# A two-layer attention and FFN kernel on one Trainium2 core: eight unread matmuls at its start, another order of the first head pair, and the fourth query projection of each grouped pair moved behind the first value products

## The reference, cut to what matters

```
x = x + xattn(layernorm(x), ctx)     # 32 heads of 128, RMS norm inside, position bias, mask, softmax; returns hidden + out
x = x + ffn(layernorm(x))            # silu(gate) * up, 1376 wide, down
x = x + grouped(layernorm(x), ctx)   # 32 query heads, 8 key/value heads, rope, 30*tanh(l/30), mask, softmax
x = x + lora(layernorm(x))           # W plus the fold of eight rank-16 pairs, bias
```

## Time and profile before

| | |
|---|---|
| runs | 1738.42, 1744.41, 1743.58 us; median 1743.58 |
| the profiled execution | 1740.23 us, its span 1738.4 us |
| mean granted TensorE clock | 0.987 |
| busy share | PE 96%, PE weight load 83%, DVE 52%, POOL 39%, ACT 37% |
| DMA | 74.99 MB, 43 GB/s over the span |

### The profile page before, as it was taken

The page is one execution under the profiler, slowest core; times in us unless marked ns, Lnnn a source line. Parts: engine busy times, 40 slices in busy tenths (PEclk is TensorE's granted clock), DMA queues, the critical chain, the costliest instruction groups (busy, mean ns, idle before and its releaser), DMA issues. The chain is left out here.

```text
span 1738.4 us, 26186 instructions
## 1 busy us (share of the span) xinstructions
PE 1677.0 (96%) x9412; PEld 1449.2 (83%) x9412; DVE 912.4 (52%) x1462; ACT 642.2 (37%) x1757; POOL 685.3 (39%) x480
## 2 busy tenths in 40 slices
PE   8899999999999999999989998799999999999997
PEld 7788888888888888888868886688888788888875
DVE  5734454443544434443454346556657556665674
ACT  5422233221332223332222222455546545564550
POOL 4532343333433324433253433445435434443524
PEclk9999999999999999999989999899999999999998
DMA  5111100111101111011011110201011110010011
GB/s 177 52 52 51 51 20 32 51 51 51 46 5 51 51 51 51 0 51 57 1 51 50 47 38 25 65 31 37 31 38 43 44 37 31 25 43 25 24 38 49
DMA packets 30898, 74.99 MB, mean 43 GB/s; under 512 B 5776, under 2 KB 10256, under 8 KB 30832
## 3 DMA queue, kind: packets, MB, share of 16 engines
q1 hardware_dynamic: 30832, 74.10, 12.2%
HBM read 71.99 MB, written 2.10 MB: 43 GB/s over the span
## 5 line engine op out<-in xcount | busy, mean ns | idle before, releaser
L1761 POOL TENSOR_TENSOR g_swapped<-g_swapped,rawB 128x512 f32<-128x512 f32 x80 | 103.5, 1295 | 159.3 <-ACT g_swapped L1545 159.3
L631 ACT COPY x_pT<-banks 128x512 f32<-128x512 f32 x64 | 37.5, 586 | 337.6 <-PE banks L485 337.6
L920 POOL TENSOR_TENSOR wtV_lo<-rawV,wtV_hi 128x1024 fp32r<-128x1024 f32 x16 | 38.5, 2406 | 309.6 <-ACT wtV_hi L643 309.6
L55 PE MATMUL banks<-wtV_hi,cT_lo 128*128 128x256 f32 x512 | 145.1, 283 | 0.0
L57 PE MATMUL banks<-wtV_hi,cT_hi 128*128 128x256 f32 x512 | 144.8, 283 | 0.0
L56 PE MATMUL banks<-wtV_lo,cT_hi 128*128 128x256 f32 x512 | 144.7, 283 | 0.0
L934 POOL TENSOR_TENSOR x_probs<-x_probs,x_inv 128x512 f32<-128x512 f32 x64 | 66.8, 1044 | 158.0 <-DVE x_inv L769 155.1
L55 PE MATMUL banks<-wtV_hi,g_att_lo 128*128 128x512 f32 x256 | 106.2, 415 | 8.1 <-DVE g_att_lo L1659 8.1
L777 DVE COPY x_v<-banks 128x512 f32<-128x512 f32 x60 | 41.5, 692 | 127.7 <-PE banks L57 127.7
L623 ACT ACTIVATE x_probs<-x_probs,x_top 128x128 f32<-128x128 f32 x256 | 99.2, 390 | 18.8 <-DVE x_top L760 18.8
L801 DVE TENSOR_TENSOR resid<-banks,resid 128x512 f32<-128x512 f32 x128 | 84.1, 686 | 40.0 <-PE banks L57 40.0
(11 more groups left out here) (226 smaller groups left out, 4953.2 us busy)
## 6 DMA issues: line engine op xcount, KB each, us to landing
rawV<-in_x_wV SPq DMA_DIRECT2D x16, 512.0 KB, 4.3
rawO<-in_x_wO SPq DMA_DIRECT2D x16, 512.0 KB, 6.0
rawO<-in_g_wQ SPq DMA_DIRECT2D x16, 512.0 KB, 3.2
rawV<-in_g_wO SPq DMA_DIRECT2D x16, 512.0 KB, 3.2
rawA<-in_x_wA SPq DMA_DIRECT2D x15, 512.0 KB, 6.3
rawB<-in_x_wB SPq DMA_DIRECT2D x15, 512.0 KB, 5.0
rawA<-in_f_gu SPq DMA_DIRECT2D x5, 512.0 KB, 3.7
rawB<-in_f_gu SPq DMA_DIRECT2D x5, 512.0 KB, 3.1
```

The lines of the kernel that those rows point to most:

```text
L55: pe.matmul(out, w[1], x[0], start=start, stop=False)
L631: nc.scalar.copy(pT[:, j, :], banks[:, TURN_BANK + j, :]).then_inc(pT_ready, 1)
L920: pool.tensor_tensor(wt[kind][1][:, :], raw[kind][:, :], f32(wt[kind][0][:, :]), ALU.subtract)\
L1761: pool.tensor_tensor(part, part, sin[:, :].unsqueeze(1).to_broadcast([P, HB, P]), ALU.mult)\
```

## The change

It has three parts. At the start, TensorE's list gets eight matmuls whose result nobody reads; the two last context chunks are cut ahead of the key weights of head 1, and the value weights ahead of the copies of the first keys; `turn_x` goes ahead of each `values_of`. In the first head pair, SyncE loads V and B ahead of the bias; `add_hidden` goes from VectorE to ScalarE (between the last `keep_values`/`high` and `exps(0, 0)`), GpSimd's `twice_of` goes ahead of the mask and gets one more operation (a sign), `inverse(0, 0)` goes ahead of `logits(0, 1)`, and GpSimd's low parts of V and B go, in every `body`, from its end behind `bias(a, 0)`. In the grouped attention, the fourth query projection goes behind `turn` 3, and the lists of ScalarE and VectorE follow.

```diff
 SyncE, first attention, body:
                     load("A", g)
-                    bias(g)
                     load("V", g)
                     load("B", g)
+                    bias(g)
                     load("O", g)
 TensorE, start:
+                def warm(n):
+                    for _ in range(n):
+                        pe.matmul(banks[:, 4, :], wqk("A", 0, 1, 0), wt["A"][0][:, half_of(1)], start=True, stop=True)
                 def start():
                     pe.wait_ge(key_hi["A"], 1)
+                    warm(WARM)                       # WARM = 8
                     pe.wait_ge(key_lo["A"], 1)
...
                     for n in range(4):
-                        values_of(n, V0 + n)
                         turn_x(2 * n)
                         turn_x(2 * n + 1)
+                        values_of(n, V0 + n)
 ScalarE, start:
                     key_half("A")
-                    context(0)
-                    context(1)
+                    for c in range(DC):
+                        context(c)
                     key_half("B")
-                    context(2)
-                    context(3)
+                    weights("V", 0)
                     for half in range(2):
                         keep(k_[:, 0, half * HALF:(half + 1) * HALF], K_A0 + half)
-                    weights("V", 0)
                     scale_x(0)
                     scale_x(1)
...
                     for n in range(4):
+                        high(2 * n)
+                        high(2 * n + 1)
                         if n < 3:
                             scale_x(2 * n + 2)
                             scale_x(2 * n + 3)
...
                         keep_values(n)
-                        high(2 * n)
-                        high(2 * n + 1)
+                    for b in range(B):
+                        add_hidden(b)                # scalar.activation(.., Identity, bias=mean_scaled, scale=twice)
 VectorE, start:
                     logits(0, 0)
-                    for b in range(2):
-                        add_hidden(b)
+                    inverse(0, 0)
                     logits(0, 1)
                     query(Q_B0, 0, 1)
-                    inverse(0, 0)
-                    for b in range(2, 4):
-                        add_hidden(b)
                     inverse(0, 1)
                     query(Q_B0 + 1, 1, 1)
-                    for b in range(4, B):
-                        add_hidden(b)
 GpSimd, start and body:
                     query_half("B")
+                    twice_of()
                     pool.wait_ge(mask_in, DMA)
...
                     bias(0, 0, True)
-                    twice_of()
...
                     weights("O", 0)
-                    weights("V", 1)
-                    weights("B", 1)
 body:
                     bias(a, 0)
+                    weights("V", g)
+                    weights("B", g)
                     normalise(a, 0)
...
                     bias(a + 1, 1)
-                    if not last:
-                        weights("V", g + 1)
-                        weights("B", g + 1)
 TensorE, grouped attention, body:
                     weights_ready("Q", p)
-                    for n in range(4):
-                        if n == 3 and not first:
-                            turn(p - 1, 0)
-                            turn(p - 1, 1)
-                        project(..n..)
+                    query(0)
+                    query(1)
+                    if not first:
+                        turn(p - 1, 0)
+                        turn(p - 1, 1)
+                    query(2)
                     if not first:
                         pe.wait_ge(proj_free, ..)
                         pv(p - 1, 0, before_kv)
                         turn(p - 1, 2)
                         pv(p - 1, 1, before_kv)
                         turn(p - 1, 3)
+                    query(3)
+                    if not first:
                         weights_ready("O", p - 1)
+                        pv(p - 1, 2, before_kv)
                         output_batch(r, u, 0)
-                        pv(p - 1, 2, before_kv)
                     scores(p, 0, rope_of(r, u, 1, 0), first)
 ScalarE, grouped attention, body:
                     for i, blk in enumerate(blocks):
+                        if i == end and not first:
+                            attn_hi(p - 1, 0)
+                            probs_hi(p - 1, 2)
+                            attn_hi(p - 1, 1)
+                            probs_hi(p - 1, 3)
                         swap(seq(r, u, blk[0]), at[i], nth[i], first)
-                        if i == end - 1:
-                            ...probs_hi 0 and 1
-                    ...attn_hi 0, probs_hi 2, attn_hi 1, probs_hi 3
+                        if i == end - 2 and not first:
+                            probs_hi(p - 1, 0)
+                            probs_hi(p - 1, 1)
 VectorE, grouped attention, body:
-                        if i and i < end:
+                        if i and i < end - 1:
                             add(i - 1)
+                        if i == end and not first:
+                            attn_lo(p - 1, 0)
+                            probs_lo(p - 1, 2)
+                            attn_lo(p - 1, 1)
+                            probs_lo(p - 1, 3)
                         rotate_cos(blk[0], at % 2, ROPES * r + at)
-                        ...the same four steps stood behind rotate_cos of the last block
+                        if i == end - 2 and not first:
+                            probs_lo(p - 1, 0)
+                            probs_lo(p - 1, 1)
+                        if i >= end - 2:
+                            add(i)
```

More of the change, by code:

```diff
@@ L672, in high, with add_hidden @@
                     nc.scalar.copy(xT[0][:, :, tok(b)], x_bank(b)).then_inc(x_hi, 1)
+                def add_hidden(b):
+                    act.wait_ge(twice_ready, 1)
+                    nc.scalar.activation(resid[:, b, :], resid[:, b, :], ACT.Identity, bias=mean_scaled[:, b:b + 1],
+                                         scale=twice[:, b:b + 1]).then_inc(hidden_added, 1)
                 def start():
                     key_half("A")
-                    context(0)
-                    context(1)
+                    for c in range(DC):
+                        context(c)
                     key_half("B")
-                    context(2)
-                    context(3)
+                    weights("V", 0)
                     for half in range(2):
                         keep(k_[:, 0, half * HALF:(half + 1) * HALF], K_A0 + half)
-                    weights("V", 0)
                     scale_x(0)
@@ L802, in output_batch @@
                         .then_inc(proj_free, 1)
[L804 to L808, removed]
                 def context(c):
@@ L960, in twice_of @@
                     pool.wait_ge(twice_steps, 2)
-                    pool.tensor_tensor(mean_scaled[:, :], core.moments[:, :, 0], core.rstd[:, :], ALU.mult).then_inc(twice_steps, 1)
+                    pool.tensor_tensor(core.var_eps[:, :], core.moments[:, :, 0], core.rstd[:, :], ALU.mult).then_inc(twice_steps, 1)
                     pool.wait_ge(twice_steps, 3)
+                    pool.tensor_scalar(mean_scaled[:, :], core.var_eps[:, :], -1.0, None, ALU.mult).then_inc(twice_steps, 1)
+                    pool.wait_ge(twice_steps, 4)
                     pool.tensor_scalar(twice[:, :], core.rstd[:, :], 1.0, None, ALU.add).then_inc(twice_ready, 1)
@@ L1478, in body, with query @@
                     weights_ready("Q", p)
[L1479 to L1482 removed]
+                    def query(n):
                         project(seq(r, u, Q_AT[u] + n), Q_AT[u] + n, "Q", n % 2, n // 2)
+                    query(0)
[4 more added lines that the diff above has]
+                    query(2)
                     if not first:
@@ L1575, in body @@
                     for i, blk in enumerate(blocks):
-                        swap(seq(r, u, blk[0]), at[i], nth[i], first)
-                        if i == end - 1:
-                            if not first:
-                                probs_hi(p - 1, 0)
-                                probs_hi(p - 1, 1)
-                    if not first:
-                        attn_hi(p - 1, 0)
-                        probs_hi(p - 1, 2)
-                        attn_hi(p - 1, 1)
-                        probs_hi(p - 1, 3)
+                        if i == end and not first:
[3 more added lines that the diff above has]
+                            probs_hi(p - 1, 3)
+                        swap(seq(r, u, blk[0]), at[i], nth[i], first)
+                        if i == end - 2 and not first:
+                            probs_hi(p - 1, 0)
+                            probs_hi(p - 1, 1)
                     if not first:
@@ L1685, in body @@
                         at = ROPE_AT[u] + i
-                        if i and i < end:
+                        if i and i < end - 1:
                             add(i - 1)
```

(17 more changed lines are left out.)

1 line of the change is left out of this document (added).

## The result

| | before | changed |
|---|---|---|
| median | 1741.90 us (4 runs, 1738.42 to 1744.41) | 1722.35 us (4 runs, 1721.07 to 1723.25) |
| ratio, 95% | | 0.9889 [0.9868, 0.9909] |
| profiled execution, its span | 1740.23, 1738.4 | 1721.07, 1719.3 |
| mean granted TensorE clock | 0.987 | 0.988 |

A forecast was written before the change was run, and what follows sets the result against it. TensorE, busy 96% of the span, was taken as the bound, so gains come from its waits and half clock. 1.5 + 0.7 + 8.0 + 9.0 = 19.2 us, placing the changed kernel at 1723 us, range 1714 to 1734.

The forecast's parts named there:

- The start: Start, up to the queries: 2.7 less two new waits of 0.6 and 0.5, taken as 1.5 us gained.
- the 0.5 us for the last transposes: End of the start: the last two transposes wait 0.5 us for their scale from GpSimd and ScalarE.
- the term of 2.7 us: Start: with the full clock from 8.3 us, the key matmuls end at 19.2 in place of 21.9.
- First head pair: Pair 0's attention: from last query to turn(0,1) 2.1 us in place of 2.8, a gain of 0.7 us.
- Rival (c): First head pair: hidden adds slow on ScalarE, deciding from 0.85 us each; 1735 us; chance 0.03.
- Pair 1: From body to output of pair 1: the 6.00 us wait and the half clock go, 8.0 us gained.
- Rival (b): Pair 1 keeps some 3 us of wait, its chain being longer than counted; 5 us lost, 1728; chance 0.12.
- The step that named two causes: Pair 1's wait: V's late load behind the bias, and VectorE's clog by the hidden adds; both removed.
- Grouped bodies: Grouped attention: each of 15 bodies loses its wait for the cut attention, 0.6 us each, 9.0 us.
- (a): Grouped bodies: the wait moves to `pv` 2 or quarter 0's cut, 0.5 us per body; 1730.5; chance 0.12.
- (d): Grouped bodies: earlier turns find probabilities not ready, 2 us each, slower at 1753; chance 0.02.
- Rival (e): Start: the eight matmuls don't raise the clock, 1.1 us less, 1724; chance 0.71 together with the forecast itself.

The follow-up runs named there:

- the repeat: The changed kernel, unaltered, measured and profiled once more: 1722.18 us, ratio 0.9888 to the kernel before.
- one pair: Changed kernel with 13 more unread matmuls in each norm, with the eight at the start and without them: 1712.89 and 1714.67 us.
- the grouped order alone: The kernel before with only the new order of the grouped bodies: 1728.98 us, ratio 0.9927.
- the first head pair's part alone: The kernel before with only the first head pair's edits (loads, hidden adds on ScalarE, inverse, GpSimd's order): 1733.62 us, ratio 0.9951.

## Why the prediction was right

Time, direction and range held. The mechanisms of pair 1 and of the grouped bodies held; that of the start held only in part, and one cost was missed. That the sum came out within 0.1 us of the span's 19.1 is in part luck.

**The start**: forecast 1.5 us, measured 1.62, but by other terms. The clock was up at the first real matmul in this profile, which came at 7.52 and not 8.2 us because the context landed earlier; in the repeat the matmul came at 7.90, the clock rose only at 10.4, and the queries still began at 35.11. The keys end at 19.0 and not 19.2, the wait for `wtV_lo` was 1.00 us and not 0.6, and the 0.5 us for the last transposes never came: the two `scale_x` end at 31.5 us and nothing waits for them. The errors cancel. And the term of 2.7 us that the rise of the clock was to give is hidden behind the value weights (but for 0.3 us in one pair): without any unread matmul the start gained 1.24 and 0.80 us, not the 0.4 named as the bound for a clock that stays low. What counts is that V is cut on landing and not behind two copies (16.13 in place of 17.12), and that the keys are done by then: their first and last matmuls start at 7.31 and 20.21 with the chunks in the new order and no unread matmul, at 7.51 and 21.59 with the grouped order alone, which has the old start.

**First head pair**: 0.79 us (2.41 - 1.62) against 0.7. Turn(0,1) waits 0.63 where 0.9 was said, the first not at all.

**The adds**: 5.76 us for eight, 0.72 each, where 0.67 was taken from a like row; ended at 42.2 with the exponentials at 43.18. Rival (c) needed 0.85.

**Pair 1**: 8.0 forecast, 7.98 measured. The slack of 1.7 us in the chain over A and the bias held (turn(1,0) starts at 61.42 without a wait, its probabilities normalised from 58.46 and 60.00 on). Rival (b) is out with it. The step that named two causes is confirmed by undoing each: 1.0 and 4.1 us alone. A forecast for either edit alone would have had to see that waits in a row hide one another, and that a short wait keeps the half clock.

**Grouped bodies**: 9.0 forecast, 11 measured in a kernel that has no other change. The mechanism stood and rivals (a) and (d) are out, but the term was mis-sized: the way from turn 3 to a wide matmul takes 0.36 us (1201.92 to 1202.28), not 0.26 + 0.26. So a body gains 1.11 - 0.36 = 0.75 us, and 15 of them 11.2. The change from the transposes to a wide matmul was put too high.

**What was missed**: the unread matmuls cost nothing at their own place and 3.1 us 1300 us later, at the return of the grouped loop (1.5 for the gap, 1.6 for the clock that fell behind it, which it doesn't in every kernel). The rows to see it by were in the profile of before: a wait of 1.63 us at that return, put down to VectorE, and the instruction queue among the DMA queues. This loss and the surplus of the grouped order nearly cancel (11.4 - 3.1 = 8.3 against 9.0), which is why the sum came out right. Rival (e), that the eight don't raise the clock before the real work, is neither in nor out: it holds in the repeat (half clock up to 10.4 us) and not in the first profile. Its price of 1.1 us is wrong, since the queries began at the same time in both. That the eight don't pay has two other reasons: the wait for V, which the sum counted with 0.6 us but which takes the whole term, and the loop's return, which no rival named.

## What to carry to other kernels

Count TensorE's instructions ahead of a hardware loop as a part of the loop's price: look at the first dozen matmuls behind each jump back for gaps put down to "issue", and at the instruction packets there, and try the loop a few instructions further on. When two waits stand in one chain, undo them together in the sum: either alone gave 1.0 and 4.1 of 8.0 us. When two profiles differ at a stage, first compare when the DMA that the stage waits for landed: here the cast that waits for it moved between 16.03 and 17.23 us, and with it the start of the queries. And where a small edit adds code to an engine's front, compare every later stage, not only the one that it was made for.

## What the hardware showed

**Code placement.** The same loop body cost 0, 2.2, 2.9, 5.2 or 6.2 us more at its return in kernels that differ in the number of matmuls ahead of it (26 or 34, then 0, 4, 8 and 12; with 26 and 34 the norms' waits differ too). The place of the second gap goes with that number. The price doesn't go with it alone: with eight ahead it was 3.6 to 5.7 us. The instruction packets are 16 KB each (10 packets, 0.16 MB). The Trainium skill, "Runtime: NRT & Kernel Launch", section "Instruction fetch mechanics", says that code comes in blocks of 16 KiB and that a taken branch whose target lies outside a window of two pages must fetch it first. The same section gives TensorE 128 KiB, eight such blocks. The traces agree with the block and with the price of a return; for TensorE they don't fit a window of two pages but do fit the eight blocks, since a pass that took 7 packets to bring was run again with none.

**The clock behind such gaps.** The changed kernel and its repeat have half clock behind the second gap (steps of 0.43 us for 3.4 us), and so has the one with the adds on VectorE (its gap is 0.4 us longer); the kernel with the bias loaded first has the same gap and no half clock. And the clock can fall behind the first gap alone: it did with the first head pair's part alone, whose TensorE program is that of the kernel before, and didn't in the kernel before, where the gap is 1.63 us. The first three lines are of the former, the last two of the kernel with the bias first:

```profile
1376.15 0.56 PE L55 MATMUL banks<-cT_hi,wtB_lo 128*128 128x512 f32 x1 [1.80 <-issue]
1376.51 0.63 PE L56 MATMUL banks<-cT_lo,wtB_hi 128*128 128x512 f32 x1
1376.93 0.63 PE L57 MATMUL banks<-cT_hi,wtB_hi 128*128 128x512 f32 x1
```

```profile
1377.39 0.51 PE L56 MATMUL banks<-cT_lo,wtB_hi 128*128 128x512 f32 x1 [1.49 <-issue]
1377.73 0.39 PE L57 MATMUL banks<-cT_hi,wtB_hi 128*128 128x512 f32 x1
```

These bodies take 40.16 us where 36.42 is usual (3.7, against 2.1 in the kernel before), and 39.34 where 35.70 is (3.6, against 5.2). So a fall of the clock costs 1.6 us at this place. What decides whether it falls isn't shown: with the grouped order alone it didn't behind a first gap of 1.91 us.

**The granted clock at the start.** The record gives 1.00 from the beginning, but the first matmuls step at 0.43 us: up to 7.5 us in the changed kernel's profile, to 10.4 in its repeat, to 12.2 in the kernel before. Up to there only the steps tell the clock. Of the six profiles with eight unread matmuls, two (the changed kernel and the adds on VectorE) were at the full clock at the first real matmul, and four rose only between 10.4 and 11.0 us.
